# Padding a 119-row weight load to 128 partitions in a one-core graph-network kernel

## What is computed

```
h  = relu(bn1(conv1(xc)))                  # 1x1 convolution, xc is x with channels first
h  = bn2(conv1d(h, conv2_w, pad=8))        # 256 in, 256 out, 17 taps along the nodes
x_conv = relu(h + xc)
A  = exp(-dist(s, s)) * adj ; x_nmp = A @ relu(x @ w_msg.T + b_msg)
gates (sigmoid, sigmoid, tanh) of [x_conv, x_nmp] @ w_ih.T and x @ w_hh.T
x  = x + (1 - z) * n + z * x
```

## Time and profile before

| | us |
|---|---|
| median of 3 runs | 1824.06 |
| lowest and highest | 1821.44, 1824.92 |
| profiled execution, its own time | 1824.12 |
| span of that execution in the profile | 1822.3 |
| granted TensorE clock, mean over the span | 0.991 |

### The profile page before, as it was taken

The page is one execution under the profiler, slowest core; times in us unless marked ns, Lnnn a source line. Parts: engine busy times, 40 slices in busy tenths (PEclk is TensorE's granted clock), DMA queues, the critical chain, the costliest instruction groups (busy, mean ns, idle before and its releaser), DMA issues. The chain is left out here.

```text
span 1822.3 us, 36602 instructions
## 1 busy us (share of the span) xinstructions
PE 1736.8 (95%) x12222; PEld 1140.1 (63%) x12222; DVE 1474.3 (81%) x3194; ACT 875.7 (48%) x1617; POOL 583.6 (32%) x744
## 2 busy tenths in 40 slices
PE   2777999999998999999999999999999999999997
PEld 1456777764444666666666666666666666666664
DVE  4778888873336888888888888888888888888886
ACT  3665565554334444444444444444444444444442
POOL 3777777730111222222222222222222222222221
PEclk9899999999999999999999999999999999999999
DMA  6197988758654343333333433433333333333331
GB/s 213 39 350 268 305 284 298 258 177 305 214 179 141 95 114 95 105 113 99 102 106 99 114 94 100 114 94 105 114 99 102 107 99 114 94 99 114 94 107 35
DMA packets 242772, 262.36 MB, mean 144 GB/s; under 512 B 82364, under 2 KB 178611, under 8 KB 242218
## 3 DMA queue, kind: packets, MB, share of 16 engines
q1 hardware_dynamic: 242712, 261.60, 46.3%
HBM read 154.57 MB, written 90.18 MB: 134 GB/s over the span
## 5 line engine op out<-in xcount | busy, mean ns | idle before, releaser
L1556 PE MATMUL ps_rz<-big 128*128 128x512 f16 x2304 | 560.2, 379 | 0.7 <-DVE big L1549 0.7
L1556 PEld LDWEIGHTS ps_rz<-big 128*128 128x128 f16 x2304 | 222.0, 98 | 203.0 <-DVE big L1549 0.9
L1556 PE MATMUL ps_n<-big 128*128 128x256 f16 x2304 | 314.2, 273 | 0.2
L1556 PEld LDWEIGHTS ps_n<-big 128*128 128x128 f16 x2304 | 225.1, 98 | 95.2 <-DVE big L1693 1.2
L1556 PE MATMUL ps_l<-big 128*128 128x512 f16 (+1 forms) x1536 | 272.1, 327 | 8.7 <-DVE big L1795 4.5
L1267 PE MATMUL m_ps<-big 128*128 128x512 f16 (+1 forms) x1152 | 268.6, 375 | 4.1 <-DVE big L1034 3.6
L1724 POOL TENSOR_TENSOR big<-big 128x256 f32<-128x256 f32 x128 | 97.5, 762 | 450.8 <-ACT big L1717 450.8
L1556 PEld LDWEIGHTS ps_l<-big 128*128 128x128 f16 x1536 | 149.9, 98 | 97.3 <-DVE big L1795 5.5
L1556 PE MATMUL ps_b<-big 128*128 128x256 f16 x1536 | 189.9, 273 | 2.1 <-DVE big L1624 2.1
L1267 PEld LDWEIGHTS m_ps<-big 128*128 128x128 f16 x1152 | 111.9, 98 | 106.3 <-DVE big L1034 2.4
L1699 ACT ACTIVATE big<-big,w_scale 128x512 f32<-128x512 f32 x128 | 92.7, 724 | 177.0 <-DVE big L1690 177.0
(11 more groups left out here) (240 smaller groups left out, 2783.9 us busy)
## 6 DMA issues: line engine op xcount, KB each, us to landing
spectra<-ysb SPq DMA_DIRECT2D x96, 256.0 KB, 2.5
big<-spectra SPq DMA_DIRECT2D x64, 384.0 KB, 3.5
xin<-in_x SPq DMA_DIRECT2D x64, 256.0 KB, 4.1
x_normed<-front SPq DMA_DIRECT2D x64, 256.0 KB, 2.9
h_turned<-front SPq DMA_DIRECT2D x64, 256.0 KB, 4.2
big<-h_turned SPq DMA_DIRECT2D x64, 256.0 KB, 2.7
big<-in_adj SPq DMA_DIRECT2D x64, 256.0 KB, 3.4
big<-in_x SPq DMA_DIRECT2D x64, 256.0 KB, 2.8
```

What stands on the lines that cost most here:

```text
L1556: last = pe.matmul(dest, stationary(dl), moving(wl), start=start and n == 0, stop=stop and n == 2, **kw)
```

## The change

The host's array of tiles gets 128 rows in place of 119. The last nine are zeros. The three loads of the tiles write all 128 partitions of `raw_a` and `raw_b`. All that reads the tiles still reads rows 0 to 118, through `raw`.

```diff
 def filter_tiles(w):
-    out = np.zeros((OT, TAPS, NT, D), w.dtype)
+    out = np.zeros((P, NT, D), w.dtype)
+    tiles = out[:OT * TAPS].reshape(OT, TAPS, NT, D)
     for t, width in enumerate(WIDTHS):
-        out[:width, :, t, :] = w[OT * t:OT * t + width].transpose(0, 2, 1)
-    return out.reshape(OT * TAPS, NT * D)
+        tiles[:width, :, t, :] = w[OT * t:OT * t + width].transpose(0, 2, 1)
+    return out.reshape(P, NT * D)
...
+        def loaded(t, n):
+            if t < IN_NEG:
+                return raw_a[:, t * D:(t + n) * D]
+            return raw_b[:, (t - IN_NEG) * D:(t - IN_NEG + n) * D]
...
-                    sp.dma_start(raw(ts[0], len(ts)), tiles_d[:, ts[0] * D:(ts[-1] + 1) * D]).then_inc(loaded_tiles[c], 16)
+                    sp.dma_start(loaded(ts[0], len(ts)), tiles_d[:, ts[0] * D:(ts[-1] + 1) * D]).then_inc(loaded_tiles[c], 16)
```

## The result

| | before | after |
|---|---|---|
| median, 5 runs each on one chip (us) | 1824.92 | 1816.68 |
| lowest and highest (us) | 1821.44, 1829.25 | 1813.56, 1817.83 |
| profiled execution's own time (us) | 1824.12 | 1816.68 |
| span of it in the profile (us) | 1822.3 | 1814.9 |
| next stage begins at (us) | 79.77 | 70.93 |

The ratio is 0.996, 95% interval 0.9944 to 0.9976: faster by 0.4%, 7.3 us of 1825, where 6.0 were forecast (1818.1 us). The profiled executions differ by 7.4 us. In the first stage alone 8.84 us were gained.

A forecast was written before the change was run, and what follows sets the result against it. TensorE, busy 95% of the span, was taken as the bound, with gains only in the first stage. Piece 1's 3.0 us plus TensorE's pause's 3.0 made 6.0, taking 1824.12 to 1818.1 us; range 1813.5 to 1822.5.

The forecast's parts named there:

- The bound: Whole kernel: TensorE busy 95% of the span; first-stage gains or losses shift everything after by as much.
- 0.44 is 7 of 16: Tile loads, first stage: a DMA share of 0.44 means 119-row loads occupy 7 of 16 engines.
- The loads: Tile loads, first stage: 327 GB/s on 16 engines; piece 0 there at 21.9 us, piece 1 at 28.3.
- The limit of 195 GB/s: Tile loads: the rate above which piece 1 (tiles 6 to 19) is on time.
- The head: Start of first stage: tiles' work begins 1.44 us earlier, less one 0.93 us hold-up of VectorE, leaving 0.5 us.
- Piece 1: Tiles 6 to 19: on time, so VectorE's low part of pair 4 starts 3.0 us earlier, head's 0.5 included.
- low 4: First stage: start of VectorE's low part of pair 4, forecast at 37.1 us in place of 40.09.
- TensorE's pause: First stage, before tile 6: the 4.24 us pause and the slow clock after it vanish, 3.0 us gained.
- The rest of the stage: First stage from 51.87 us on: VectorE sets the pace as before, nothing gained, one long low part kept.
- No faster loads: Rival, tile loads: they get no faster or not enough, under 195 GB/s, 1824 or 1825.7 us; chance 0.06.
- The port: Rival, first stage: GpSimd takes the gain back from VectorE through the shared SBUF port, 1823.7 to 1825.4 us; chance 0.12.
- The clock: Rival, first stage: TensorE stays at the lower clock level, slower, up to 1839 us; chance 0.03.

The follow-up runs named there:

- e1: Tiles padded to 120 rows and loaded with 120 partitions, against the changed kernel's 128; profiled execution 1815.79 us.
- e4: The kernel before, without padding, each piece loaded as two DMAs of 112 and 7 rows; profiled execution 1817.04 us.
- e2: Tiles padded to 121 rows and loaded with 121 partitions, against the changed kernel's 128; profiled execution 1819.03 us.
- e11: The changed kernel run again, nothing altered; median of 7 1815.68 us, ratio to the kernel before 0.9959.
- e5: Only piece 1 (tiles 6 to 19) loaded with 128 partitions, the other pieces with 119 as in the kernel before; profiled execution 1817.32 us.
- e6: Only piece 0 (tiles 0 to 5) loaded with 128 partitions, the other pieces with 119 as in the kernel before; profiled execution 1823.92 us.
- e7: Changed kernel with GpSimd's pairs 7 to 17 made to wait so its cast and subtraction run beside VectorE's low parts; profiled execution 1821.13 us.
- e8: Changed kernel with GpSimd's wait three tiles later, so its subtraction lies clear of VectorE's low parts; profiled execution 1819.27 us.
- e9: Changed kernel with each piece loaded as two DMAs, rows 0 to 63 and 64 to 127; profiled execution 1818.71 us.

## Why the prediction was right

*The bound.* "0.44 is 7 of 16" is shown by e1 to e4. That the first stage's gain passes through to the end held within the 5 us by which the later stages vary. The prediction named a longer second stage or a longer rest as a sign of being wrong; they were 1.5 us longer, too little to tell.

*The loads.* I put 327 GB/s, from the seven engines' pace. It was 403 to 444 with 128 rows, near the upper bound. The pieces landed 0.9 and 1.9 us earlier than worked out. It changed nothing, since both were on time already. The limit of 195 GB/s was set too high for VectorE and TensorE, and said nothing of GpSimd: at about 165 GB/s (e2) the low part of pair 4 and TensorE were on time to within 0.8 us, but GpSimd was late enough to meet VectorE later.

*The head.* 1.44 us less one hold-up of 0.93 was the sum. Against the kernel before, ScalarE started 1.0 us earlier, `row_scale` being 0.41 us later in this profile (24.84 against 24.43; in e11 it was at 24.04). L411 took 0.69 us in place of 0.47, so it was held up by 0.2 us, not 0.93. The hold-up came behind it: one of the small instructions, on two columns, took 1.15 us (L422 at 31.98) beside GpSimd's subtraction. It was hidden, as VectorE had waited 0.85 us there for the result of tile 0 before the change, and now had no such wait. TensorE began tile 0 at 31.48 for 32.27: 0.79 us gained where 0.5 were forecast. That is 1.44 - 0.41 - 0.22. The sum came near because two errors met, a hold-up 0.7 us too long and a `row_scale` that was 0.41 us later; the second is chance.

*Piece 1.* 3.37 us gained up to low 4, where 3.0 were forecast: right, and e5 and e6 show the pieces by themselves.

*TensorE's pause.* The pause went, and the slow clock with it: 3.26 us gained, 3.0 forecast. Its counterpart is e6, where the pause stays and with it the whole 39.55 us.

*The rest of the stage.* Here the size was off. The sum had nothing (one long low part kept); 1.92 us were gained, and 0.30 in the period that I had left alone. 1.24 of the 1.92 is the long low part, which is gone, and 0.6 are two others, at 51.87 and 64.17 before (1.09 and 1.25 us), which now took 0.86 and 0.87. I had GpSimd drift against VectorE, 3.8 us for a cycle against 4.1. Before, it did: VectorE's low part of each pair came 0.48 us behind the start of GpSimd's scaling at first (40.09 against 39.61), and 1.99 us behind at 68.41 (against 66.42). That is past the scaling and into the subtraction. After, at pairs 4 and 8 the difference is -0.10 and 0.29, and GpSimd's scaling is itself lengthened where they meet (2.08 and 1.94 us for 1.83). This is the term that the sum lacked. Each gives way a little, GpSimd's cycle becomes about 3.9 us, and it is done at 60.45, before the drift gets it to the subtraction. That position is the cause is shown by e7 and e8. In e1, e2, e4, e5 and e9 GpSimd began pair 3 1.1 to 6.1 us later than it could have; each had a low part of 1.65 to 2.10 us, and then the two engines fell into step again, with low parts of 0.86 to 0.90 at the end. This cost 0.6 to 2.1 us against the changed kernel. So the changed kernel's good position is worth up to 2 us, and that it got it is luck: nothing in the prediction says at which point of GpSimd's cycle the low parts would fall.

*The rivals.* No faster loads: excluded by the windows. The port: real, and its price per pair about right (1.22 put, 1.0 to 1.1 in e7), but it did not happen in the changed kernel. All six would have left a gain of about 2.5 us in the stage (8.84 less e7's 6.3). Nor did each low part wait for a scaling, which would have left 0.4: five of the six before 59 us took 0.86 to 0.88. The clock: 1.00 in every window from 10 to 58 us.

*The time.* 6.0 forecast; 8.84 in the stage, 7.4 between the profiled executions, 7.3 by the ratio. The step that was mis-sized is the last part of the stage: nothing put, 1.92 measured. The whole time came nearer to the forecast than the stage did only because the later stages of this profile were 1.5 us longer.

## What to carry to other kernels

Look at the DMA share, not only at the rate: a share that stands still at a fraction of 16 (0.44, 0.25) says that a transfer runs on few engines, and then its row count is what to change, by padding or by splitting off the rest. Ask for a late transfer only whether it is on time for its first reader on every engine: here 165 GB/s were enough for VectorE, and cost 2 us through GpSimd, which began its work late (in e1 a like delay cost 0.6). Where two engines hold each other up, the time depends on how their cycles lie to each other, and a change far from them can move that: by up to 2 us beside a gain of 8.8 here, without anything in the work of the two being touched.

## What the runs showed of the hardware

- The pace of one DMA engine was not constant: 20 GB/s in a 119-row load (7 engines), 13 to 14 in a 120-row one (15), 25 to 28 in a 128-row one (16), and 12 to 14 in a 64-row one (16, e9). A share of 1.0 can mean 200 or 440 GB/s.
- Five more rows (124 for 119) made a load slower by more than a third (143 to some 90 GB/s), and the kernel by 19.5 us.
- A VectorE instruction on two columns, 0.23 us in the kernel before, took 1.15 us beside GpSimd's subtraction. A `SCALAR_TENSOR_TENSOR` of 256 columns, 0.47 us by itself, took 1.38 beside a subtraction, 0.80 beside a cast and 0.69 beside a scaling.
- GpSimd loses too: its scaling of two tiles, 1.83 us, took up to 2.10 where VectorE's low part began beside it.
- The last two stages, with the same instructions in each of the thirteen profiles, took 1741.1 to 1745.8 us.
